# A GNN stack: a fill of a spare tile ahead of each group's gathers, and the spline weights moved from PSUM to SBUF

## The chip, the cores and the metric

The kernel runs on one core of one Trainium2 chip. The time is the device time of one execution in microseconds (us). The engines are PE (TensorE), DVE (VectorE), ACT (ScalarE), POOL (GpSimd) and SP (SyncE, which here only issues transfers).

## The reference, cut to what matters

A graph with N = 12500 nodes of 64 features and E = 200000 edges, sorted by destination, passes through four residual layers:

```python
h = relu(layernorm(x)); x = x + L0(h)  # spline convolution: every edge has 8 weights,
                                       # msg = sum_k w[e,k] * (h[src] @ W[k]); mean over dst; batch norm; elu
h = relu(layernorm(x)); x = x + L1(h)  # graph attention: softmax over the edges of a dst node of
                                       # leaky_relu(xl[src] + xr[dst]) @ att, weighted sum of xl[src]
h = relu(layernorm(x)); x = x + L2(h)  # three graph convolutions: normalised sum of h[src] over dst
h = relu(layernorm(x)); x = x + L3(h)  # mean of h[src] over dst, joined with h, one product
```

The 8 weights of an edge are the products of three pairs (1 - f, f), one pair for each of its three attributes.

## The kernel before, in words

The edge list is cut into 392 groups of 512 edges (J = 4 columns of 128). For a group, POOL issues four indirect transfers (L544). Each takes 128 row numbers from a column of `idx_block` in SBUF and brings 128 rows of a table in DRAM into one slot of the ring `gath`, which has S = 8 slots. PE then multiplies the rows with one-hot matrices, which sum them by destination tile (128 nodes). A group and tile pair is a visit; a group has one visit or a few.

The passes over the groups follow one another:

- The spline pass (`spline_tab`, 392 groups). DVE forms `hat2` (L1139, 16 columns), from it the 8 weights `hat8` (L1142, 32 columns), and then z = rows times weights (L1147, 2048 columns), which goes to SBUF. z reads the gathered rows from SBUF and `hat8` from PSUM. Then come the visits: DVE makes four one-hot tiles (L1118), PE multiplies (L800, L803, L808), DVE adds the results.
- The attention pass (`gat_tab`, 392 groups). Each visit is a chain over PE, DVE and ACT (L1258 makes its one-hot tile).
- Four sum passes (`sum_tab`, 168 groups each, 672 in all). Here the other 224 groups are covered by a dense matrix of edge counts: SP loads panels of it, and PE multiplies them (L909, L910) between the visits (L893). DVE makes the visits' one-hot tiles with L1343 (two inputs in SBUF) and adds the sums (L1324, L1327).

That dense matrix is filled on the way: 900 indirect accumulating transfers (L518, "scatters") are issued by POOL, 36 for every 28 groups, between the gathers of the spline pass from its 113th group on and of the attention pass. Each waits until the previous one has landed.

The order on POOL: before a group's first gather it waits until its slot is free (`slot_free`, L540). DVE gives a slot back at the end of a group (`free_slot`, L1051, an empty instruction), always that of four groups ago. So when group g is done, POOL may issue the gathers of group g + 4. Every 28 groups POOL copies the next row numbers (L503) and, where there are scatters, their cells and counts (L509, L510). POOL's sequencer handles waits ahead of the engine, so that instructions lie ready behind one another.

```python
pool.wait_ge(slot_free[s], pool_count)                       # 541
for j in range(J):
    nc.gpsimd.indirect_dma_start(out=dest[:, s, j, :], ...)  # 544, then_inc(gathered[s], 16)
    if cells and (j == J - 1 or j == 1 and hi - lo == 2):
        scatter(...)                                         # 518
```

Of the kernel before, what the change touches and what calls it, by code (L numbers as in the profile page):

```python
# [5 lines left out]
def gnn_stack_kernel(  # L6
# [19 lines left out]
    P = 128  # L26
# [3 lines left out]
    KS = W0.shape[0]  # L30
# [3 lines left out]
    J = 4  # L34
# [12 lines left out]
    NBLK = NG // BG  # L47
# [11 lines left out]
    NX = 1  # L59
# [22 lines left out]
    gat_tab = nc.dram_tensor("gat_tab", (T * P, 2 * F), fp32).ap()  # L82
    sum_tab = nc.dram_tensor("sum_tab", (T * P, 3 * F), bf16).ap()
# [6 lines left out]
    with ctx:  # L90
        def sb(name, shape, dt=fp32):
            return ctx.enter_context(nc.sbuf_tensor(name, shape, dt))
# [4 lines left out]
        def sem(name):  # L97
            return ctx.enter_context(nc.semaphore(name))
# [5 lines left out]
        R = sb("R", [P, T * F])  # L104
# [56 lines left out]
        o = 2 * J * KS * F  # L161
        zt = R[:, o:o + GE]
        o += GE
        hat2 = R[:, o:o + 4 * J].rearrange("p (j a b) -> p j a b", a=2, b=2)
        o += 4 * J
        cell_a, times_a = R[:, o:o + DP].bitcast(i32), R[:, o + DP:o + DP + DP // 2].bitcast(fp16)
        lists = [A[:, k * DC:(k + 1) * DC].bitcast(i32) for k in range(2 * TWIN + 1)]
        work = [R[:, k * DC:(k + 1) * DC] for k in range(5)] + [hT[:, (TWIN - 1) * P:(TWIN - 1) * P + DC]]
# [5 lines left out]
        o = SD * GE  # L174
# [8 lines left out]
        count_block = sb("count_block", [P, 2 * SB], fp16)  # L183
        dense_i = sb("dense_i", [1, 2], i32)
        fold = sb("fold", [P, F])
        floor = sb("floor", [P, 1])
        neg_max = sb("neg_max", [P, 1])
        diff = sb("diff", [P, 1])
# [27 lines left out]
        psCD = pb("psCD", 1024)  # L216
        psC, psD = psCD[:, 0:512], psCD[:, 512:1024]
        psE = pb("psE", 1024)
        hat8 = psB[:, 0:KS * J].rearrange("p (j a b) -> p j a b", a=2, b=4)
        ps_turned, ps_product = (psA, psB), (psCD, psE)  # L220


# [31 lines left out]
        zero_ready = sem("zero_ready")  # L254
        zeroed = sem("zeroed")
        cells_ready = sem("cells_ready")
        cells_moved = sem("cells_moved")
        cells_copied = sem("cells_copied")
        scattered = sem("scattered")
# [94 lines left out]
        def registers(eng, name, n):  # L354

            regs = [eng.alloc_register(f"{name}{k}") for k in range(n)]
            for r in regs:
                eng.reg_mov(r, 0)
            return regs
# [120 lines left out]
        def _(pool):  # L480
# [39 lines left out]
                    in_=count_block[:, c:c + 1], in_offset=None, compute_op=ALU.add,  # L520
                ).then_inc(scattered, 16)

            def edge_loop(table, dest, first, last, cells=None):

                block0 = cells[2] if cells else 0
                with pool.Fori(first, last) as i:
                    for h in range(2):
                        for k in range(BG):
                            s = (h * BG + k) % S
                            if k == S:  # L530

                                copy_block(1 - h, i * 2 + (h + 1))
                                if cells:
                                    copy_cells(cells[0], cells[1], (block0 + h + 1) % 2, i * 2 + (block0 + h + 1))
                            pool.reg_add(pool_count, pool_uses, (h * BG + k) // S + 1)
                            if s >= LAG:
                                pool.reg_add(pool_count, pool_count, pool_early)
                            pool.wait_ge(loaded_edges, 16 * 9)
                            pool.wait_ge(block_copied, pool_copied)
                            pool.wait_ge(slot_free[s], pool_count)  # L540
                            lo, hi = k * SB // BG, (k + 1) * SB // BG
                            for j in range(J):
                                c = h * BC + k * J + j
                                nc.gpsimd.indirect_dma_start(  # L544
                                    out=dest[:, s, j, :], out_offset=None, in_=table,
                                    in_offset=bass.IndirectOffsetOnAxis(ap=idx_block[:, c:c + 1], axis=0),
                                ).then_inc(gathered[s], 16)
                                if cells and (j == J - 1 or j == 1 and hi - lo == 2):
                                    scatter((block0 + h) % 2 * SB + (hi - 1 if j == J - 1 else lo))
                    pool.reg_add(pool_uses, pool_uses, 2 * BG // S)  # L550
# [24 lines left out]
            pool.wait_ge(table_ready, 48)  # L575
            copy_block(0, 0)
            pool.reg_add(pool_early, pool_early, 1)
            edge_loop(gat_tab, gath_gat, 0, NBLK // 2, (cell_b, times_b, n + NX))
            _, first_block = dense_range(pool, "pool")
            with pool.Fori(0, 3) as layer:  # L580
                copy_block(0, first_block * 2)
                wait_apart(pool, pool_count, table_ready, layer * (16 * NS) + (48 + 16 * NS))
                pool.reg_add(pool_early, pool_early, 1)
                edge_loop(sum_tab, gath_sum, first_block, NBLK // 2)
            copy_block(0, first_block * 2)
            pool.wait_ge(table_ready, 48 + 4 * 16 * NS)
            pool.reg_add(pool_early, pool_early, 1)
            edge_loop(sum_tab, gath_sum, first_block, NBLK // 2)


        @block.scalar
# [366 lines left out]
        def _(dve):  # L958
# [62 lines left out]

            dve.wait_ge(rows_stored, 16)
            V.memset(A[P - 32:P, 2 * DC:(2 * TWIN + 1) * DC].bitcast(i32), FAR).then_inc(lists_clear, 1)
            for semaphore in slot_free + bc_free + [prod_t, prod_t] + panel_used + [dense_added, dense_folded]:
                V.engine_nop().then_inc(semaphore, 1)

            asked = [0]
# [435 lines left out]
```

## Time and profile before

| | us |
|---|---|
| median of 3 runs | 12690.88 |
| lowest and highest run | 12641.61, 12698.97 |
| the profiled execution: its own time | 12644.07 |
| its span | 12642.2 |
| PE busy | 8810.2 (70%) |
| POOL busy | 7247.4 (57%) |
| DVE busy | 4847.3 (38%) |
| ACT busy | 1810.1 (14%) |

The spline pass lies at 136 to 3835 us of the span, the attention pass at 4091 to 7668, and the sum passes at 7846 to 8955, 9066 to 10174, 10279 to 11379 and 11468 to 12569. Busy time leaves out waits, register work and the sequencers. Idle time of an engine is put down to what ended it: "DVEq L1051" is a slot given back, "issue" is idle time for which no event shows, and "remote" or "another core or an unknown queue" is an event whose source the profile can't name.

### The profile page before, as it was taken

Reading aid. Unit: us, or ns where it says so; the run is one execution under the profiler, and the core shown is the slowest. Engines: PE = TensorE matmul, PEld = TensorE weight load, DVE = VectorE, ACT = ScalarE, POOL = GpSimd, SP = SyncE. Lnnn points to the kernel's source line nnn. Section 1 sums busy time; section 2 is a strip of 40 time slices with the busy share of each in tenths; the row PEclk is TensorE's granted clock in tenths of the full one; section 3 lists DMA queues with packets and bytes.
Section 4 is the critical chain, followed back from the end, with each engine's and each line's share of the span. In section 5 each row is a group of like instructions: output and inputs, shape, how many; then the busy total and the mean of one; then the engine's idle time right before and its main releaser. Section 6 shows DMA issues by size and latency. Waiting matters only on the chain.

```text
span 12642.2 us, 197864 instructions
## 1 busy us (share of the span) xinstructions
PE 8810.2 (70%) x46558; PEld 6095.1 (48%) x46559; DVE 4847.3 (38%) x11847; ACT 1810.1 (14%) x4731; POOL 7247.4 (57%) x6848
## 2 busy tenths in 40 slices
PE   4787777778784666666667764788378747864885
PEld 4787777777774444555555553222222222221222
DVE  5554444444446233333333334222322232234223
ACT  0000000000001233333333332000000000000000
POOL 3446665655554776666666662556455545664664
PEclk8888888888886677777777786888588868876887
DMA  7401111111111322222222221444244424433443
GB/s 286 155 17 14 14 13 13 13 13 13 12 12 25 62 61 60 59 60 58 57 56 56 56 54 38 146 148 150 57 149 151 137 77 146 154 115 105 149 153 90
DMA packets 577485, 1013.05 MB, mean 80 GB/s; under 512 B 342921, under 2 KB 352440, under 8 KB 577331
## 3 DMA queue, kind: packets, MB, share of 16 engines
q1 hardware_dynamic: 258819, 724.21, 17.0%
q0 software_dynamic: 316112, 286.92, 12.9%
q14 instruction: 138, 1.13, 0.0%
q10 hardware_dynamic: 2400, 0.53, 0.0%
q8 instruction: 16, 0.26, 0.0%
HBM read 862.36 MB, written 148.79 MB: 80 GB/s over the span
## 4 chain that ended last, share of the span: by engine, by line
PE 34%; another core or an unknown queue 31%; issue 15%; DVE 7%; DVEq 4%; DMA 3%; ACT 3%; SPq 1%; ACTq 1%; POOL 0%; POOLq 0%
PE psAB L800 13%; PE psCD L910 4%; PE psCD L909 4%; DMA R<-dense 2%; PE psCD L808 2%; PE psAB L853 2%; PE psCD L866 2%; PE psAB L859 1%; DVE one_hot L1118 1%; PE psCD L844 1%; ACT Q L702 1%; PE psAB L850 1%; PE psCD L781 1%; PE psAB L893 1%
## 5 line engine op out<-in xcount | busy, mean ns | idle before, releaser
L544 POOL DMA_INDIRECT gath<-sum_tab,idx_block x2688 | 2669.2, 993 | 2201.8 <-issue 1154.8
L800 PE MATMUL psAB<-one_hot,R 128*128 128x128 f32 x15680 | 2424.4, 316 | 633.6 <-DVE one_hot L1118 317.0
L800 PEld LDWEIGHTS psAB<-one_hot,R 128*128 128x128 f32 x15680 | 2254.6, 221 | 707.7 <-issue 658.2
L544 POOL DMA_INDIRECT gath<-spline_tab,idx_block x1568 | 1502.0, 958 | 1542.0 <-DVEq L1051 1058.1
L544 POOL DMA_INDIRECT gath<-gat_tab,idx_block x1568 | 1541.2, 983 | 1023.2 <-DVEq L1051 579.7
L909 PE MATMUL psCD<-R,Q 128*128 128x512 f16 x3528 | 1505.2, 427 | 563.3 <-DMA R<-dense 493.7
L518 POOL DMA_INDIRECT dense<-count_block,cell_block x900 | 1496.3, 1663 | 424.2 <-issue 268.8
L910 PE MATMUL psCD<-R,Q 128*64 128x512 f16 x3528 | 1555.3, 441 | 17.2 <-issue 17.1
L1343 DVE SCALAR_TENSOR_TENSOR R<-iota_row,tile_base,dstf 128x512 f32 x928 | 705.1, 760 | 1168.3 <-issue 1168.3
L893 PE MATMUL psAB<-gath,R 128*128 128x192 bf16 x3712 | 508.2, 276 | 822.7 <-DVE R L1343 406.6
L1324 DVE TENSOR_REDUCE row_part<-psAB 128x64 f32 x940 | 331.7, 353 | 1855.9 <-PE psAB L893 756.8
L1118 DVE TENSOR_SCALAR one_hot<-iota_row,tile_base,dstf 128x128 fp32r<-128x128 f32 x1952 | 602.7, 354 | 1115.8 <-remote 676.5
L909 PEld LDWEIGHTS psCD<-R,Q 128*128 128x128 bf16 x3528 | 343.5, 97 | 1424.7 <-issue 1424.0
L1263 DVE CUSTOM_DVE_ANT_0 Q<-psAB,Q 128x512 f32<-128x512 f32 x492 | 340.0, 691 | 1548.6 <-remote 1110.0
L866 PEld LDWEIGHTS psCD<-gath,Q 128*128 128x128 f32 x3936 | 597.5, 222 | 686.2 <-issue 685.8
L1147 DVE TENSOR_TENSOR R<-gath,psAB 128x2048 f32<-128x2048 f32 x392 | 896.2, 2286 | 18.6
L910 PEld LDWEIGHTS psCD<-R,Q 128*64 128x64 bf16 x3528 | 387.1, 110 | 962.4 <-issue 962.4
L850 PE MATMUL psAB<-one_hot,xr_hi 128*128 x492 | 301.1, 612 | 782.5 <-ACT xr_lo L691 420.9
L866 PE MATMUL psCD<-gath,Q 128*128 x3936 | 589.1, 300 | 308.6 <-issue 171.4
L893 PEld LDWEIGHTS psAB<-gath,R 128*128 x3712 | 311.7, 101 | 1015.8 <-issue 996.3
L853 PEld LDWEIGHTS psAB<-ident,gath 128*128 128x128 f32 x3936 | 714.1, 255 | 65.8 <-issue 0.5
L853 PE MATMUL psAB<-ident,gath 128*128 128x128 f32 x3936 | 709.4, 340 | 0.3 <-issue 0.3
(252 smaller groups left out, 9263.1 us busy)
## 6 DMA issues: line engine op xcount, KB each, us to landing
R<-dense SPq DMA_DIRECT2D x504, 896.0 KB
dense<-stage SPq DMA_DIRECT2D x126, 896.0 KB
Q<-dst_rows SPq DMA_DIRECT2D x392, 256.0 KB
gath<-sum_tab,idx_block POOLq DMA_INDIRECT x2688
gath<-spline_tab,idx_block POOLq DMA_INDIRECT x1568
gath<-gat_tab,idx_block POOLq DMA_INDIRECT x1568
sum_tab<-Q SPq DMA_DIRECT2D x28, 672.0 KB, 5.5
dense<-count_block,cell_block POOLq DMA_INDIRECT x900
```

Of the source, the lines that this page charges most:

```text
L518: nc.gpsimd.indirect_dma_start(out=dense, out_offset=bass.IndirectOffsetOnAxis(ap=cell_block[:, c:c + 1], axis=0), in_=count_block[:, c:c ...
L544: nc.gpsimd.indirect_dma_start(out=dest[:, s, j, :], out_offset=None, in_=table, in_offset=bass.IndirectOffsetOnAxis(ap=idx_block[:, c:c + ...
L800: nc.tensor.matmul(block, z[:, w, j, k * P:(k + 1) * P], oh32[:, j, :], start=(j == 0), stop=(j == J - 1))
L850: nc.tensor.matmul(psA[:, pair], xr_hi[:, :], onehot, start=True, stop=False)
L853: ins = nc.tensor.matmul(psA[:, bass.ds((v & 1) * GE + j * P, P)], gath_gat[:, s, j, :], ident[:, :], start=False, stop=(j == J - 1))
L866: ins = nc.tensor.matmul(psD[:, 0:F], prT[:, j * P:(j + 1) * P], gath[:, bass.ds(o + j * P, F)], start=(j == 0), stop=(j == J - 1))
L893: ins = nc.tensor.matmul(psAB[:, ring(v, 0, SV, 512, 3 * F)], oh16[:, bass.ds((v & (SV - 1)) * GE + j * P, P)], gath_sum[:, s, j, :], star ...
L909: nc.tensor.matmul(psC, tile[:, 0:2 * F], counts, start=first_one, stop=last_one)
L910: ins = nc.tensor.matmul(psD[0:F, :], tile[:, 2 * F:3 * F], counts, start=first_one, stop=last_one)
L1118: V.tensor_scalar(oh32r[:, j, :], iota_row[:, :], tile_base[:, bass.ds(t, 1)], dstf[:, bass.ds(chunk_col + j, 1)], ALU.add, ALU.is_equal). ...
L1147: V.tensor_tensor(z[:, s % 2, :, :].rearrange("p j (k f) -> p j k f", f=F), gath_spline[:, s, :, :].unsqueeze(2).to_broadcast([P, J, KS, F ...
L1343: V.scalar_tensor_tensor(oh16[:, ring(v, 0, SV, GE)].rearrange("p (j n) -> p j n", j=J), iota_row[:, :].unsqueeze(1).to_broadcast([P, J, P ...
```

## The change

- A new tile `spacer` (128 x 256, fp32, SBUF) and a semaphore `spacer_set`, which starts at 1.
- In the attention pass and the sum passes POOL fills this tile with zeros once per group, after the wait for the slot and before the group's four gathers. It waits first for the fill of the group before (`spacer_set` against a register that counts up). The tile is read by nobody.
- `hat8` moves from PSUM (`psB`) to SBUF (`R`, behind `hat2`); the lists behind it in `R` shift by 32 columns.

```diff
-        o += 4 * J
+        hat8 = R[:, o + 4 * J:o + 12 * J].rearrange("p (j a b) -> p j a b", a=2, b=4)
+        o += 12 * J
...
+        spacer = sb("spacer", [P, 256])
...
-        hat8 = psB[:, 0:KS * J].rearrange("p (j a b) -> p j a b", a=2, b=4)
...
+        spacer_set = sem("spacer_set")
...
+            (pool_spaced,) = registers(pool, "pool_spaced", 1)
+
-            def edge_loop(table, dest, first, last, cells=None):
+            def edge_loop(table, dest, first, last, cells=None, spaced=False):
...
                             lo, hi = k * SB // BG, (k + 1) * SB // BG
+                            if spaced:
+                                pool.reg_add(pool_spaced, pool_spaced, 1)
+                                pool.wait_ge(loaded_edges, 16 * 9)
+                                pool.wait_ge(spacer_set, pool_spaced)
+                                nc.gpsimd.memset(spacer[:, :], 0.0).then_inc(spacer_set, 1)
...
-            edge_loop(gat_tab, gath_gat, 0, NBLK // 2, (cell_b, times_b, n + NX))
+            edge_loop(gat_tab, gath_gat, 0, NBLK // 2, (cell_b, times_b, n + NX), spaced=True)
...
-                edge_loop(sum_tab, gath_sum, first_block, NBLK // 2)
+                edge_loop(sum_tab, gath_sum, first_block, NBLK // 2, spaced=True)
...
-            edge_loop(sum_tab, gath_sum, first_block, NBLK // 2)
+            edge_loop(sum_tab, gath_sum, first_block, NBLK // 2, spaced=True)
...
-            for semaphore in slot_free + bc_free + [prod_t, prod_t] + panel_used + [dense_added, dense_folded]:
+            for semaphore in slot_free + bc_free + [prod_t, prod_t] + panel_used + [dense_added, dense_folded, spacer_set]:
                 V.engine_nop().then_inc(semaphore, 1)
```

## Rows read from the trace of the kernel before

**Rows 1.** The page: busy time by engine, and the shares of the chain by engine.

```profile
PE 8810.2 (70%) x46558; PEld 6095.1 (48%) x46559; DVE 4847.3 (38%) x11847; ACT 1810.1 (14%) x4731; POOL 7247.4 (57%) x6848
...
PE 34%; another core or an unknown queue 31%; issue 15%; DVE 7%; DVEq 4%; DMA 3%; ACT 3%; SPq 1%; ACTq 1%; POOL 0%; POOLq 0%
```

**Rows 2.** Windows of two passes: length, busy us of PE, PEld, DVE, ACT, POOL.

```profile
136.00:3835.00 3699.00, 2901.42 (x21437) 2806.28 (x21438) 1804.16 (x4123) 338.75 (x976) 2094.95 (x1965) 0.85 0.19 45
...
7846.00:8955.00 1109.00, 796.29 (x2824) 285.71 (x2824) 296.25 (x686) 9.65 (x18) 669.74 (x679) 0.80 0.43 133
```

**Rows 3.** Windows of line L1147 (z) alone: DVE busy (count).

```profile
200.00:900.00 700.00, 210.34 (x92) 0.88 0.39 145
1000.00:3800.00 2800.00, 633.49 (x278) 0.84 0.12 13
```

**Rows 4.** Waits of POOL, 1000 to 3800: us in total, times, longest.

```profile
POOL gath L544 <- DVEq L1051: 742.0, 179, 11.2
```

**Rows 5.** The page: gathers of the three kinds of pass, busy us, mean ns | idle before.

```profile
L544 POOL DMA_INDIRECT gath<-sum_tab,idx_block x2688 | 2669.2, 993 | 2201.8 <-issue 1154.8 <-DVEq L1051 958.0 <-DMA sum_tab<-Q 89.0
...
L544 POOL DMA_INDIRECT gath<-spline_tab,idx_block x1568 | 1502.0, 958 | 1542.0 <-DVEq L1051 1058.1
L544 POOL DMA_INDIRECT gath<-gat_tab,idx_block x1568 | 1541.2, 983 | 1023.2 <-DVEq L1051 579.7 <-issue 411.0 <-DMA dense<-count_block,cell_block 31.7
```

**Rows 6.** Line L544: who waited for its gathers (us, times).

```profile
  PE psAB L893: 240.7, 15
  PE psCD L844: 25.5, 1
```

**Rows 7.** DVE groups by form: busy us, mean ns | idle before.

```profile
L1147 DVE TENSOR_TENSOR R<-gath,psAB 128x2048 f32<-128x2048 f32 x392 | 896.2, 2286 | 18.6
...
L1142 DVE TENSOR_TENSOR psAB<-Q,R 128x32 f32<-128x32 f32 x392 | 79.0, 202 | 55.9 <-issue 0.2
...
L1139 DVE TENSOR_TENSOR R<-Q 128x16 f32 x392 | 68.4, 175 | 179.8 <-issue 179.7
...
L1039 DVE TENSOR_TENSOR R<-X,s 128x6272 f32<-128x6272 f32 x4 | 26.8, 6692 | 0.1
...
L1387 DVE TENSOR_TENSOR H<-R,Q 128x896 f32<-128x896 f32 x21 | 22.5, 1085 | 0.4
```

**Rows 8.** Timeline, start of the attention pass: start us, us, engine, line.

```profile
4091.74 1.04 POOL L544 DMA_INDIRECT gath<-gat_tab,idx_block  x1 [0.80 <-POOL idx_block L503]
4092.01 6.69 DVE L1228 TENSOR_TENSOR R<-R,H 128x6272 f32<-128x6272 f32 x1 [5.55 <-ACT H L615]
4093.08 6.47 POOL L544 DMA_INDIRECT gath<-gat_tab,idx_block  x1 [0.30 <-issue]
```

**Rows 9.** Timeline, one group of the spline pass: z and the first gather.

```profile
2059.93 2.29 DVE L1147 TENSOR_TENSOR R<-gath,psAB 128x2048 f32<-128x2048 f32 x1
2059.95 0.98 POOL L544 DMA_INDIRECT gath<-spline_tab,idx_block  x1 [0.69 <-issue]
```

**Rows 10.** Line L492: the only fill of 128 x 256 on POOL.

```profile
L492 POOL MEMSET hT<- x1: 313/313/313, 2.1 to 2.1; 128x256 f32 x1
```

**Rows 11.** Timeline of POOL, second sum pass: a copy queued behind a gather.

```profile
9480.55 0.29 POOL L503 COPY idx_block<-srci 128x112 int32 x1
```

**Rows 12.** Timeline of POOL, attention pass: a copy and the gather behind it.

```profile
5128.49 0.79 POOL L510 COPY count_block<-Q 128x36 f16 x1
5129.75 1.01 POOL L544 DMA_INDIRECT gath<-gat_tab,idx_block  x1 [0.47 <-issue]
```

**Rows 13.** Waits of PE in 7846 to 7880, the head of the first sum pass.

```profile
PE psAB L893 <- DMA gath<-sum_tab,idx_block: 47.8, 4, 34.8
```

**Rows 14.** Line L1258 (attention pass): ns min/median/max.

```profile
L1258 DVE TENSOR_SCALAR one_hot<-Q,node_no x488: 485/486/848, 4113.7 to 7661.6; 128x512 f32 x163
```

**Rows 15.** Line L1343 (two inputs in SBUF, sum passes): ns min/median/max.

```profile
L1343 DVE SCALAR_TENSOR_TENSOR R<-iota_row,tile_base,dstf x928: 750/751/822, 7840.7 to 12572.8; 128x512 f32 x186
```

**Rows 16.** Waits of DVE, 1000 to 3800.

```profile
DVE one_hot L1118 <- remote: 528.2, 233, 8.4
```

## The prediction

> **What bounds the kernel now.** I read the busy times first, then the chain that ended last, then windows of the passes, and last the waits of POOL and of those who need its gathers. PE is busy 70% of the span and is the largest single part of the chain, with 34%; the next is 31% of events without a known source, then 15% "issue". POOL, the engine that the change loads, is busy 57% and has 0% of the chain [rows 1]. So what counts is how much idle time POOL has in each pass, and whether anybody waits for gathers.
>
> In the spline pass POOL is busy 2095 of 3699 us, in the first sum pass 670 of 1109 [rows 2]. With scatters running, z comes every 2800/278 = 10.1 us, before them every 700/92 = 7.6 us [rows 3]. In the stretch with scatters POOL waited 742.0 us for a slot given back, 742.0/278 = 2.67 us per group [rows 4]. In the sum passes it waited 958.0 us over 672 groups, 1.43 us each; in the attention pass 579.7 us over 392 groups, 1.48 us each [rows 5]. These three are POOL's slack. In the whole span PE waited for a gather 16 times [rows 6], and z stood idle before its start for 18.6 us over 392 groups, with no gather named [rows 7]. The gathers run ahead: group g + 4 is issued when g is done, so three whole groups (some 30 us with scatters) lie between issue and use.
>
> **The change, part by part.**
>
> *hat8 in SBUF, the instructions themselves.* L1142 writes 32 columns to PSUM in 202 ns; L1139 writes 16 columns to SBUF in 175 ns. The slope of a product with both inputs in SBUF is (6692 - 1085)/(6272 - 896) = 1.043 ns per column [rows 7], so 16 columns more make 192 ns: 10 ns saved, 392 times, on DVE's path, -4 us. At most it falls to 175 ns, -11 us; at least it stays, 0. z: from the same two rows, 2048 columns with all inputs in SBUF would take 1085 + 1152 x 1.043 = 2287 ns; it takes 2286 ns now [rows 7]. So 0; a start held by a running gather is bounded below.
>
> The Trainium skill says otherwise: its page "Perfetto Trace Analysis", section "Optimizing Scalar/DVE Operations", gives a DVE operation about 60 ns of access overhead on SBUF and about 125 ns on PSUM. By it both instructions would lose 65 ns, an estimate of 392 x 2 x 0.065 = 51 us saved. The row of z bears out none of that, and I go by the row.
>
> *hat8 in SBUF, what it does to POOL.* Now z has one input in SBUF; afterwards it has two. What two do is seen at the start of the attention pass: L1228, both inputs in SBUF, ran from 4092.01 for 6.69 us; a gather begun at 4093.08, inside it, took 6.47 us where its neighbour, begun before it, took 1.04 [rows 8]. The gather ended at 4099.55, 0.85 us after L1228, so it was held at a point about 0.1 us behind its start (0.96, the mean of the spline pass [rows 5], less 0.85). Beside z it isn't held now: a gather begun 0.02 us after z took 0.98 us [rows 9]. Afterwards it will be: it waits until z ends, 2.29 - 0.02 - 0.10 = 2.17 us. POOL issues in order, so one z holds one instruction of POOL: at most 2.17 us a group, at least 0 (POOL idle). Where POOL comes from one gather to the next every 1.25 us, the mean is nearer 2.17 - 0.6 = 1.6. I take 1.6 and keep 2.17 as the bound. Both are below the slack of 2.67 us, so POOL still waits for slots, and 30 us lie between issue and use against 7.4 (its 10.07 us per group less 2.67) + 2.17 of work, which leaves 20 us for the landing: z has its rows in time. Cost on the path: 0. The cover gone, it would be what exceeds 2.67, times 280 groups.
>
> The page "SBUF — State Buffer" of the Trainium skill, section "Who interferes with whom", states the same contention (two SBUF inputs on DVE against a GpSimd instruction that reads SBUF), and that issue order decides who blocks. By the second half z could be the one held; that is the first rival below.
>
> *The fill.* POOL gets 392 + 672 = 1064 fills of 128 x 256. The one such fill in the trace took 0.31 us [rows 10]. A copy behind a gather starts with no gap [rows 11]; from the end of a copy (5129.28) to the gather behind it is 0.47 us [rows 12], where gather to gather is 0.30 [rows 8]. So a fill adds 0.31 to 0.48 us; the short copies queued beside others took 0.79 [rows 12], which is my upper bound. The register wait is for a fill long done, and the sequencer handles it ahead. I take 0.45 us: 479 us more work for POOL. Behind the fill in POOL's queue are the group's four gathers and the scatters; for the gathers waits PE.
>
> In the attention pass 0.45 stands against a slack of 1.48, and PE waited once for a gather: 0. In the sum passes it stands against 1.43. There it shows only where PE lives from hand to mouth: at the head of each pass, where POOL starts from nothing and PE waits for each of the first four groups [rows 13]. The fourth is late by four fills: 4 x 0.45 = 1.8 us per pass, 7 us in four passes (5 to 13 by the bounds). Behind it the dense panels keep PE busy and POOL catches up.
>
> *The fill against DVE.* L1258 takes 486 ns, but up to 848: it is sometimes held, as I take it by an instruction of POOL, the held gather the other way round [rows 14]. A fill of 0.31 us falls on it in about (0.49 + 0.31)/7.3 = 11% of visits (the pass's 3577 us over 488 visits are 7.3), half of it lost: 392 x 0.11 x 0.2 = 9 us at most, 0 at least; I take 4. L1343 varies by 72 ns at most over 928 times [rows 15]: 0.
>
> *Sum.* -4 + 0 + 7 + 4 = +7 us, against the profiled execution's own 12644.07 (span 12642.2 and 1.9 around it). That execution is 0.4% below the median of the runs, 12690.88; put on the median, 12,698.
>
> **The rivals.**
>
> *z is held by the gathers (slower).* Place: L1147. If z can't start while an instruction of POOL is running, it waits for its rest. POOL is busy 57% of the spline pass [rows 2], and half of a gather or scatter is about 0.55 us: 0.57 x 0.55 = 0.31 us per z, 392 x 0.31 = 123 us: 12,821. For it: L1258's 848 ns [rows 14]. Against it: L1343, which has two inputs in SBUF as z will have, ran 928 times beside a POOL busy 60% [rows 2] and never took more than 822 ns, median 751 [rows 15]. It decides from 63/392 = 0.16 us per z on.
>
> *The fill is dear (slower).* If wait, fill and restart of the gathers come to 1.6 us, more than the slack, POOL becomes the bound: (1.6 - 1.43) x 672 + (1.6 - 1.48) x 392 = 161 us: 12,859. Against it are all rows of fills and copies.
>
> *The unknown stalls move.* Between 1000 and 3800 DVE waited 528 us in one of its lines for events without a source [rows 16], and a group costs 10.1 - 7.6 = 2.5 us more than before the scatters, 280 times, 700 us [rows 3]. Whatever disturbs the engines runs beside POOL's transfers. The held gathers move out of z into the time between groups, and the fills spread the gathers. If a tenth of the 700 us goes, -70 us: 12,628; if a tenth comes on top, 12,768. No row says which.
>
> *The change does nothing*, since z isn't in the way of a gather: the time stays as forecast, and only the trace shows it.
>
> **How the numbers follow.** Forecast (with the case that nothing happens) 58%; z held 12%; fill dear 5%; stalls fewer 15%; stalls more 10%. About 0.5%, 63 us, is what a measurement can tell from no change. Faster: 15%. Within: 58%. Slower: 12 + 5 + 10 = 27%. The range 12,620 to 12,830 takes in the bounds of the sum (-11 to +33 us), both cases of moved stalls and a held z, and leaves out the dear fill and worse.
>
> **What would show it.** hat8: L1142 at 175 to 202 ns, z at 2286 ns; slower than 2350 speaks for the first rival. Gathers of the spline pass: the mean up from 958 ns to about 958 + 1600/4 = 1360, with single ones above 3 us, and POOL's wait for slots in 1000 to 3800 down from 742 us to about 300. If that wait is near zero and z waits for gathers, the cover was thinner than I reckon. Fills: 1064 at 0.31 us, POOL's wait for slots down by about 0.45 us per group in the later passes, PE's waits for gathers still at the heads only. A change of any pass's length by over 60 us proves the sum wrong.

## The result: faster by 3.35% where the forecast said no change

| | before | after |
|---|---|---|
| median, us | 12694.67 (4 runs) | 12253.02 (4 runs) |
| lowest, highest | 12641.61, 12698.97 | 12229.47, 12295.55 |
| profiled execution: span | 12642.2 | 12293.6 |

The ratio is 0.9665, 95% interval 0.9627 to 0.9704. The forecast was 12,698 us and its range ended at 12,620.

Later jobs put the kernel before at 12,444, 12,629, 12,422, 10,209 and 12,439 us. Numbers of different jobs are compared here as ratios to the kernel before in the same job, or as passes of kernels of one job. The fourth job turned the verdict round: there the same change ran at 1.0687. Both signs have to be explained.

The page after, busy time and the chain's shares, answers to [rows 1]:

```profile
PE 8694.3 (71%) x46558; PEld 6005.2 (49%) x46559; DVE 4817.1 (39%) x11847; ACT 1804.7 (15%) x4731; POOL 8130.3 (66%) x7912
...
another core or an unknown queue 28%; PE 24%; issue 13%; DVE 5%; DMA 3%; DVEq 3%; ACT 3%; ACTq 1%; SPq 1%; POOL 0%; POOLq 0%
```

POOL has 883 us more work, and the kernel ends 349 us earlier in the profiled executions. Windows of the changed kernel (columns as in [rows 2]): the spline pass, a stretch inside it, the first sum pass.

```profile
135.00:3451.00 3316.00, 2760.68 (x21433) 2697.31 (x21434) 1774.44 (x4126) 338.33 (x974) 2631.79 (x1965) 0.90 0.21 50
1000.00:3400.00 2400.00, 1991.02 (x15271) 1942.71 (x15270) 1206.24 (x2872) 241.06 (x694) 1946.65 (x1429) 0.89 0.14 15
7455.00:8572.00 1117.00, 798.46 (x2836) 290.44 (x2836) 298.92 (x697) 9.65 (x18) 724.04 (x846) 0.79 0.43 132
```

The spline pass, 3699 us before [rows 2], is 383 us shorter: all of the gain and more. PE does the same instructions there in 2761 us in place of 2901, at a granted clock of 0.90 in place of 0.85: it spends more of the pass at the upper of its two levels. The attention pass ran 3559 us (before 3577), the sum passes 1117, 1108, 1128 and 1127 (1117, 1113, 1107 and 1106). A pass is measured here in every kernel from its first gather to the last work on its own groups; for the first sum pass before that gives 8 us more than the window of [rows 2].

The groups of the page after that answer to [rows 5], [rows 7] and [rows 10], and the fills:

```profile
L553 POOL DMA_INDIRECT gath<-spline_tab,idx_block x1568 | 1973.9, 1259 | 629.0 <-issue 536.7
...
L553 POOL DMA_INDIRECT gath<-gat_tab,idx_block x1568 | 1528.9, 975 | 456.7 <-issue 441.4
...
L550 POOL MEMSET spacer<- 128x256 f32 x1064 | 483.9, 455 | 1647.2 <-DVEq L1060 1165.9
...
L1156 DVE TENSOR_TENSOR R<-gath,R 128x2048 f32<-128x2048 f32 x392 | 900.1, 2296 | 437.4 <-DMA gath<-spline_tab,idx_block 423.2
```

The gathers are held as forecast (958 ns before, 1259 now), and z isn't. But z now waits 423.2 us for its rows, and POOL hardly waits for slots any more. Who waited in 1000 to 3400 us of the spline pass, before:

```profile
POOL gath L544 <- DVEq L1051: 620.6, 152, 11.2
DVE one_hot L1118 <- remote: 475.0, 205, 8.4
...
DVE A L1126 <- remote: 268.6, 114, 4.2
```

and after:

```profile
DVE R L1156 <- DMA gath<-spline_tab,idx_block: 379.5, 106, 6.7
...
DVE one_hot L1127 <- remote: 154.8, 94, 7.5
...
DVE A L1135 <- remote: 101.4, 51, 4.1
...
POOL gath L553 <- DVEq L1060: 24.6, 10, 3.4
```

The two waits "remote" fell from 744 to 256 us. They are what the change took away, and the waits for gathers are the largest of DVE's waits now.

**What such a wait is.** The timeline of the kernel before, one visit (start, us, engine, line):

```profile
2004.11 0.95 POOL L544 DMA_INDIRECT gath<-spline_tab,idx_block  x1 [0.30 <-issue]
...
2005.01 1.13 DVE L1118 TENSOR_SCALAR one_hot<-iota_row,tile_base,dstf 128x128 fp32r<-128x128 f32 x4
2005.01 1.08 PE L808 MATMUL psCD<-w_spline,R 128*128 128x64 f32 x8
2005.37 1.62 POOL L518 DMA_INDIRECT dense<-count_block,cell_block  x1 [0.30 <-issue]
...
2007.29 0.99 POOL L544 DMA_INDIRECT gath<-spline_tab,idx_block  x1 [0.30 <-issue]
2008.21 0.22 DVE L1126 TENSOR_TENSOR A<-A,psCD  x1 [2.07 <-remote]
2008.28 0.17 ACT L660 ACTIVATE edge_count<-psE  x1 [6.00 <-remote]
```

L1126 adds what L808 made. L808 ended at 2006.09 and DVE was free at 2006.14; the addition starts at 2008.21. PE meanwhile went on with the next visit's products (L800 from 2005.93 on). PE's release reached DVE some 2 us late, while POOL issued one transfer behind the other. I call this a late release. The trace also records the update of the semaphore itself: in the late visits it lies 0.33 us ahead of L1126 (median). So the delay is between PE's product and the update, as far as the profile's modelled ends of the products can tell.

To count them I took from each trace, for every visit with scatters running (from 1000 us to the end of the spline pass), the time from the later of "L808 done" and "DVE's previous operation done" to the start of L1126 (0.15 to 0.2 us is the mean where nothing is late; "over 1 us" is late, and the median of the late ones before is 2.1 us):

```
kernel, in the order of the text          visits  sum us  mean us  over 1 us
before                                     373     387     1.04     42%
after                                      359     165     0.46     18%
hat8 in SBUF alone (e1)                    357     131     0.37     17%
late fills alone: spline pass as before    371     308     0.83     42%
gathers behind z (e3)                      384     307     0.80     30%
one fill of 1280 per group (e4)            363     103     0.28     12%
four fills of 320 (e6)                     366      71     0.19      3%
wait for landing (e7)                      380     382     1.00     44%
four fills on one partition (e11)          367     113     0.31     13%
four tiny fills (e16)                      372     303     0.81     38%
all passes split (e10)                     358      56     0.16      1%
job at 10,209 us: tiny fills (e12)         338      69     0.20      0%
job at 10,209 us: the change (e15)         352      54     0.15      0%
```

This is one wait of several in a visit, so the sums are a gauge, not the whole cost.

When a release is late shows if the same visits are sorted by what POOL was doing at the moment that DVE could have gone on. "Paused" means more than 0.4 us behind the end of POOL's last transfer. The other columns give the time since the first transfer behind such a pause. A transfer that is held (a gather of over 1.2 us, a scatter of over 1.9) counts as a pause until 0.96 us before its end. The numbers are late visits of all:

```
kernel                              paused     under 2 us    2 to 4 us     over 4 us
before                             0 of 163      7 of 9      77 of 114     71 of 84
wait for landing (e7)              0 of 150     10 of 16     72 of 109     85 of 102
gathers behind z (e3)              0 of 96       6 of 134     5 of 30     106 of 121
one fill of 1280 per group (e4)    0 of 69       0 of 159    11 of 70      31 of 62
after                              0 of 7        0 of 230     2 of 30      62 of 89
four fills of 320 (e6)             2 of 31      10 of 278     0 of 54         none
four fills on one partition (e11)  4 of 33      39 of 144     1 of 132      2 of 55
job at 10,209 us: e12              0 of 4        0 of 10      0 of 2        0 of 319
```

In the first five rows nothing is late with POOL paused, and over 4 us into a train 50 to 88% of the visits are (before has too few under 2 us to tell). In `after` 98% of the gaps between two transfers are the usual 0.30 us, so the pause that counts there lies inside the held gather. The rule isn't sharp: in e11 visits under 2 us are late too, and in the 112 groups ahead of the scatters e4 has 15 late of 30 under 2 us.

### The profile page after: what moved, and what is told of

Read it like the earlier page. It is cut to its first block, busy times and chain, and to the rows that moved or that the text cites. A ratio compares the mean times of both kernels' runs of the same rounds, so it can differ in the third digit from the quotient of the medians.

```text
span 12293.6 us, 201058 instructions
## 1 busy us (share of the span) xinstructions
PE 8694.3 (71%) x46558; PEld 6005.2 (49%) x46559; DVE 4817.1 (39%) x11847; ACT 1804.7 (15%) x4731; POOL 8130.3 (66%) x7912
## 4 chain that ended last, share of the span: by engine, by line
another core or an unknown queue 28%; PE 24%; issue 13%; DVE 5%; DMA 3%; DVEq 3%; ACT 3%; ACTq 1%; SPq 1%; POOL 0%; POOLq 0%
PE psAB L809 5%; PE psCD L919 4%; PE psCD L918 4%; DMA R<-dense 3%; PE psAB L862 2%; PE psCD L875 1%; PE psAB L868 1%; ACT Q L711 1%; PE psCD L817 1%; PE psCD L853 1%; PE psAB L783 1%; PE psCD L790 1%; PE psE L790 1%; PE psAB L859 1%
## 5 line engine op out<-in xcount | busy, mean ns | idle before, releaser
L809 PE MATMUL psAB<-one_hot,R 128*128 128x128 f32 x15680 | 2318.7, 309 | 480.2 <-DVE one_hot L1127 374.3
L809 PEld LDWEIGHTS psAB<-one_hot,R 128*128 128x128 f32 x15680 | 2170.2, 214 | 528.2 <-issue 503.7
L553 POOL DMA_INDIRECT gath<-spline_tab,idx_block x1568 | 1973.9, 1259 | 629.0 <-issue 536.7
L520 POOL DMA_INDIRECT dense<-count_block,cell_block x900 | 1549.6, 1722 | 418.4 <-issue 272.4
L550 POOL MEMSET spacer<- 128x256 f32 x1064 | 483.9, 455 | 1647.2 <-DVEq L1060 1165.9
L1156 DVE TENSOR_TENSOR R<-gath,R 128x2048 f32<-128x2048 f32 x392 | 900.1, 2296 | 437.4 <-DMA gath<-spline_tab,idx_block 423.2
```

Source lines behind the costliest of these rows:

```text
L520: nc.gpsimd.indirect_dma_start(out=dense, out_offset=bass.IndirectOffsetOnAxis(ap=cell_block[:, c:c + 1], axis=0), in_=count_block[:, c:c ...
L550: nc.gpsimd.memset(spacer[:, :], 0.0).then_inc(spacer_set, 1)
L553: nc.gpsimd.indirect_dma_start(out=dest[:, s, j, :], out_offset=None, in_=table, in_offset=bass.IndirectOffsetOnAxis(ap=idx_block[:, c:c + ...
L809: nc.tensor.matmul(block, z[:, w, j, k * P:(k + 1) * P], oh32[:, j, :], start=(j == 0), stop=(j == J - 1))
L1156: V.tensor_tensor(z[:, s % 2, :, :].rearrange("p j (k f) -> p j k f", f=F), gath_spline[:, s, :, :].unsqueeze(2).to_broadcast([P, J, KS, F ...
```

## The experiments

The theory at the end: where releases come late, they do so beside POOL's indirect transfers issued without a pause; a pause in the issuing, whether POOL is held or fills a tile in it, takes the lateness away from the visits just behind it. Rivals on the way: the freed PSUM, no gather beside z, the fills' writes, any instruction between two transfers.

**The two parts alone (first job; before 12,444 us).** e1 takes the first hunks of the diff, e2 the rest.

```diff
-        hat8 = psB[:, 0:KS * J].rearrange("p (j a b) -> p j a b", a=2, b=4)
+        hat8 = R[:, o + 4 * J:o + 12 * J].rearrange("p (j a b) -> p j a b", a=2, b=4)
```

> Only hat8 moves to SBUF, no fills. The spline pass of the changed kernel was 382 us shorter, the later passes together were a few tens of us longer. If the move of the weights carries the whole gain (all three theories below say so), this kernel is at about 12,694 - 440 = 12,250 to 12,260, with a spline pass of about 3,316 us, and is not slower than the changed kernel. If the fills carry part of it, it is clearly above 12,300. Theories on why the move helps: (beside) POOL's transfers no longer run beside z and the turn of the group behind it; (PSUM) z no longer reads PSUM for 2.3 us; (pace) POOL as a whole is slower and its transfers come later.

> Only the fills, hat8 stays in PSUM. By the prediction's sum the fills cost 7 us at the heads of the sum passes and up to 9 by holding L1258: 12,700. If the fills spread the gathers to advantage, it is below 12,640. The spline pass has none and stays at 3,700 us.

e1: 12113.91 us, ratio 0.9742 (0.9701 to 0.9784), spline pass 3297 us against 3643 in e2, whose spline pass is the one of before. e2: 12348.05 us, 0.9929 (0.9906 to 0.9952), attention pass 3409 us against 3457 to 3465 in the three others of the job. The product of both, 0.967, is the whole change: the parts are independent, and three quarters come from `hat8`.

**Gathers kept away from z (first job).** `hat8` stays in PSUM; POOL issues the gathers of group g + 4 only when z of group g + 1 is done, and no longer as soon as group g is.

```diff
+                            if behind_z:
+                                pool.reg_add(pool_z, pool_z, 1)
+                                pool.wait_ge(loaded_edges, 16 * 9)
+                                pool.wait_ge(z_ready, pool_z)
```

> The kernel before (hat8 in PSUM, no fills), but POOL issues the first gather of a group of the spline pass only when z of the next group is done, not when the slot is given back 0.7 us ahead of z. So the first gather of a group that waited for its slot doesn't run beside z, with no port in play. (beside): most of the 382 us of the spline pass go. (PSUM): nothing goes, 3,700 us stay, or the pass is a little longer, since gathers come 2.5 us later. (pace): a part goes.

12573.99 us, 1.0119 (1.0076 to 1.0163), spline pass 3790 us. POOL waited for z, and DVE no less for late releases (before: 475.0 us in the same stretch):

```profile
POOL gath L550 <- DVE R L1153: 632.5, 127, 14.7
DVE one_hot L1124 <- remote: 620.8, 349, 9.2
```

That the first gathers no longer overlap with z isn't the gain.

**One long fill per group in the spline pass (first job).** `hat8` stays in PSUM.

```diff
+                                nc.gpsimd.memset(one_hot[:, GE:GE + 1280].bitcast(fp32), 0.0).then_inc(spacer_set, 1)
...
-            edge_loop(spline_tab, gath_spline, 0, S0)
+            edge_loop(spline_tab, gath_spline, 0, S0, spaced=True)
```

> The kernel before with hat8 in PSUM, and a fill of 1280 columns (about 1.2 us, as much as z held POOL per group in the changed kernel) ahead of each group's gathers in the spline pass alone. POOL is as slow as in the changed kernel, but its transfers run beside z as before. (pace): the spline pass falls towards 3,316 us. (PSUM): it stays near 3,700. (beside): it stays near 3,700, or falls by the part of first gathers that the fill moves out of z (the fill starts with z and takes half of it).

12139.47 us, 0.9761 (0.9719 to 0.9803), spline pass 3341 us. A fill that nobody reads does nearly what `hat8` in SBUF did (e1: 3297 us), with 1.465 us per group where the hold in e1 cost (1278 - 958) x 4 = 1.28. So neither the place of `hat8` nor z's own speed is needed for the gain; what both edits have in common is a pause in POOL's train.

**The kernel before against itself (second job; before 12,629 us).**

> The kernel before, unchanged, profiled on this chip, as the base for the lengths of the passes. Ratio 1.00. The runs so far left one theory (breaks): while POOL issues indirect transfers without a break for more than some 2 us, PE's signals reach the other engines late; a break lets them through. By it, the first line to look at is the wait of DVE's L1118 for events without a source, 676 us in the profile of before.

1.0008 (0.9991 to 1.0025); spline pass 3704, attention pass 3595, sums 1107 to 1111 us.

**Four short fills (second job).** The 1280 columns in four, one ahead of each gather.

```diff
+                                if spaced:
+                                    at = GE + j * 320
+                                    nc.gpsimd.memset(one_hot[:, at:at + 320].bitcast(fp32), 0.0).then_inc(spacer_set, 1)
```

> hat8 in PSUM, spline pass only: the 1280 columns of fill of the run before are cut into four fills of 320, one ahead of each gather. POOL gets the same extra work, some 1.3 us per group, but no gap between two transfers is longer than about 0.9 us. (pace): as good as one fill of 1280, a ratio of 0.976. (breaks, one long one needed): less, 0.98 to 1.00. (breaks, what counts is the share of time in transfers): as good or better.

12200.92 us, 0.9652 (0.9628 to 0.9676), spline pass 3220 us: 484 us shorter than e5. Late releases nearly vanish, and z waits for gathers:

```profile
DVE R L1157 <- DMA gath<-spline_tab,idx_block: 388.2, 126, 6.1
...
DVE one_hot L1128 <- remote: 51.1, 54, 4.6
```

**A pause between groups, not between transfers (second job).** `hat8` stays in PSUM, and in the spline pass POOL waits until the gathers of the group before have landed.

```diff
+                            if landed and p >= 0:
+                                if p % S == 0:
+                                    pool.reg_add(pool_landed, pool_landed, 16 * J)
+                                pool.wait_ge(loaded_edges, 16 * 9)
+                                pool.wait_ge(gathered[p % S], pool_landed)
```

> hat8 in PSUM, no fills, spline pass only: POOL issues a group's gathers only when those of the group before have landed. So every group's four gathers are a run of their own, with a pause of some 2 us behind it in which POOL does nothing. (breaks): the pause is as good as a fill, the spline pass falls to about 3,340 us, ratio 0.975. If only work on POOL helps, or if it is the port, the ratio is 1.00. If it makes POOL the bound (5 + 2.5 + 2 us per group against 10), the pass is at 3,500 to 3,700 with z waiting for gathers.

12673.06 us, 1.0029 (1.0011 to 1.0048), spline pass 3718 us, late releases as before (505.4 us):

```profile
DVE one_hot L1126 <- remote: 505.4, 225, 8.7
```

The edit didn't bring the pause that it was meant to bring. With scatters running POOL paused over 0.4 us ahead of 213 of 284 groups, 773 us in all, where e5 did so ahead of 213 of 277, 804 us in all: the wait for the landing took the place of the wait for the slot. So e7 shows that transfers still under way don't matter, but not whether an idle pause does what a fill does. Nor is it the sum of the pauses that counts: e4 has only 493 us of them and few late releases. There the fill moved the train: 228 of 360 visits fell into a pause or its first 2 us, in e7 166 of 377.

**Longer fills in the later passes (second job; e9 in the third, before 12,422 us).** The change with 704 columns in place of 256, then the same in four parts.

```diff
-        spacer = sb("spacer", [P, 256])
+        spacer = sb("spacer", [P, 704])
```

```diff
+                                if spaced:
+                                    nc.gpsimd.memset(spacer[:, j * 176:(j + 1) * 176], 0.0).then_inc(spacer_set, 1)
```

> The changed kernel with fills of 704 columns instead of 256 in the attention and sum passes, about 0.7 us in place of 0.31 to 0.45. (breaks): longer breaks free more of the stalls while POOL still has slack there (1.4 us per group), 20 to 100 us less than the changed kernel's ratio of 0.967. (fills only cost): 4 passes x 4 groups x 0.3 us and more, a few us to some tens slower than 0.967.

> hat8 in SBUF as in the changed kernel; in the attention and sum passes the 704 columns of the long fill are cut into four fills of 176, one ahead of each gather of the group. POOL's added work per group is about the same (4 x about 0.4 us against about 1.0). Theory (unbroken trains of POOL's transfers make the other engines' releases late, and every gap counts): spreading the gaps helps more than one gap per group; ratio to before 0.92 to 0.935 against 0.938 with one long fill, attention pass below 3301 us. Rival (what helps is that POOL has less idle time or is held back once per group, however it is spread): 0.938 +- 0.004. Rival (extra instructions of POOL cost by their number): above 0.945.

e8: 11868.46 us, 0.9384 (0.936 to 0.9409); attention pass 3301 us against 3595 in e5, sums 4336 against 4438. e9: 11744.52 us, 0.9468 (0.9442 to 0.9493); attention pass 3235 against 3445 in e11, sums 4232 against 4381. So the fills were far too short for what they could do, and the expectation for e9 was missed. The two ran in different jobs, so which form is better in the later passes isn't settled: each against a kernel of its job whose later passes are those of before, the split one saved less in the attention pass (210 us against 294) and more in the sum passes (149 against 102). Such unaltered passes differ within one job by up to 66 us over the four sum passes (e1, e3, e4), so the second difference says nothing.

**Fills that write almost nothing, and all passes split (third job).** e11 is e6 on one partition; e10 has `hat8` in PSUM and a fill ahead of every gather.

```diff
-                                    nc.gpsimd.memset(one_hot[:, at:at + 320].bitcast(fp32), 0.0).then_inc(spacer_set, 1)
+                                    nc.gpsimd.memset(one_hot[0:1, at:at + 320].bitcast(fp32), 0.0).then_inc(spacer_set, 1)
```

> The kernel with four short fills in the spline pass (ratio 0.965), each fill on one partition in place of 128: the same duration, 1/128 of the bytes written. Theory (the gap in time between transfers counts): 0.965 +- 0.004, spline pass about 3220 us. Rival (the fill's writes to SBUF, its lock of the port or its hold on DVE count): near 1.00, spline pass near 3700 us.

> hat8 stays in PSUM as before; one fill ahead of each gather everywhere: 320 columns in the spline pass, 176 in the attention and sum passes. Theory (gaps): spline pass about 3220 us as with the four short fills alone, attention pass as in the kernel with hat8 in SBUF and split fills; ratio about 0.925. Rival (hat8 in SBUF is needed for the gain in the attention pass too, or parts are not additive): above 0.945.

e11: 11912.66 us, 0.9592 (0.9566 to 0.9618), spline pass 3158 us. e10: 11630.46 us, 0.9371 (0.9349 to 0.9393), spline pass 3174 us, attention pass 3230. The spline pass of e11 is that of e10 with 1/128 of the bytes written in it, so the writes aren't what works; the pause between the transfers grew in both, from 0.30 us to 0.52 in e11 and 0.55 in e10 (median between two gathers). e4's one fill per group took 574 us of POOL's time in all, e11's four took 654: the spline pass is 3341 us with the one and 3158 with the other, at nearly the same time before (12,444 and 12,422). One pause per transfer does more than one per group, as far as two jobs can be compared.

**Tiny fills, and the later passes again (fourth job; before 10,209 us).**

```diff
-                                    nc.gpsimd.memset(one_hot[0:1, at:at + 320].bitcast(fp32), 0.0).then_inc(spacer_set, 1)
+                                    nc.gpsimd.memset(one_hot[0:1, at:at + 16].bitcast(fp32), 0.0).then_inc(spacer_set, 1)
```

> The kernel with four fills on one partition in the spline pass (0.959, fills of 417 ns), each cut from 320 columns to 16, so that it lasts some 100 ns. Theory (length of the gap between two transfers counts): the gap shrinks by about 0.3 us of about 0.5, so much less than the full gain: ratio 0.975 to 0.99, spline pass 3400 to 3600 us. Rival (any instruction of POOL's own between two transfers breaks the train, its length does not matter): 0.96, spline pass about 3160 us.

> The kernel with one fill of 704 columns per group in the attention and sum passes and hat8 in SBUF, again, beside the split one on the same chip. Theory (every gap counts): about 0.955 here, slower than the split fills (0.947 on its chip) by 0.5 to 1.5%. Rival (the late passes gain by POOL's added time per group, not by the number of gaps): the same as the split kernel within 0.3%.

> The same with the 704 columns in four fills of 176, one ahead of each gather, again. Both theories: 0.947 as before if this is the same chip; the theory of gaps wants it below the kernel with the long fill, attention pass at 3235 us against 3300 or more, the rival wants them equal.

> The changed kernel unaltered, on the chip of the others. Its two parts alone came to 0.9742 and 0.9929 on one chip, product 0.967; both together 0.9665 on another. Parts independent: 0.967 +- 0.005 here too. If the parts get in each other's way or the gain depends on the chip: above 0.975 or below 0.96.

e12: 10225.08 us, 1.0014 (1.0004 to 1.0023). e13: 11303.34, 1.1073 (1.1054 to 1.1091). e14: 11258.45, 1.1028 (1.1009 to 1.1046). e15: 10907.92, 1.0687 (1.0669 to 1.0705). I had expected none of this. No late release shows in this job's traces; e12, which is the kernel before but for 356 us of tiny fills, shows the same step as above like this:

```profile
2000.14 1.62 POOL L519 DMA_INDIRECT dense<-count_block,cell_block  x1 [0.30 <-issue]
...
2001.70 1.14 DVE L1128 TENSOR_SCALAR one_hot<-iota_row,tile_base,dstf 128x128 fp32r<-128x128 f32 x4
2001.71 1.08 PE L818 MATMUL psCD<-w_spline,R 128*128 128x64 f32 x8
2002.07 0.99 POOL L554 DMA_INDIRECT gath<-spline_tab,idx_block  x1 [0.27 <-issue]
...
2003.14 0.22 DVE L1136 TENSOR_TENSOR A<-A,psCD  x1 [0.30 <-PE psCD L818]
```

The product is done at 2002.79, DVE is free at 2002.84, the addition starts at 2003.14. The windows of z in the stretch with scatters, e12 and e15 (DVE busy, count):

```profile
1000.00:2800.00 1800.00, 539.35 (x236) 0.95 0.16 17
```

```profile
1000.00:3300.00 2300.00, 579.98 (x253) 0.88 0.14 15
```

A group takes 1800/236 = 7.63 us without the change and 2300/253 = 9.09 with it. POOL never waits for a slot in either stretch: it sets the pace, and each held gather costs its full length (mean 966 ns in e12, 1290 in e15). The tiny fills of e12 cost no pace, since they fit into the 0.30 us between two transfers. e14 took 45 us less than e13, but where nothing is late this doesn't test the theory of gaps. The spline pass is 3260 us against 2781, +479; the attention pass 3089 against 3020; the sum passes 3571 against 3441. Together +678 us, of 676 between the two spans.

**The repetition (fifth job; before 12,439 us).**

> Four fills of 16 columns on one partition in the spline pass, again. If the kernel before takes about 10,210 us here, as beside the last runs (no late releases at all in the trace), the ratio is 1.00 again and nothing is told. If it takes 12,400 to 12,700 us (late releases): theory (the length of the gap counts) 0.975 to 0.99; rival (any instruction between two transfers is enough) 0.96.

> The changed kernel. Theory (the change gains only where releases come late, since it takes them away, and costs where they do not): 1.069 where the kernel before takes 10,210 us, 0.967 to 0.975 where it takes 12,400 to 12,700 us. Rival (the ratios differ for another reason, as the chip's number): 0.967 or 1.069 whatever the kernel before takes.

> One fill ahead of each gather everywhere, hat8 in PSUM. Where the kernel before takes 12,400 to 12,700 us: 0.93 to 0.937, with spline pass near 3170 us. Where it takes 10,210 us POOL sets the pace of nearly all passes and the fills cost their full length: about 2781 + 392 x 4 x 0.4 = 3400 us would be the most for the spline pass, with the time at 1.09 to 1.12 of before.

e16, the tiny fills: 12397.15 us, 0.9976 (0.9956 to 0.9996), spline pass 3633 us, and late releases are there again (its waits, 1000 to 3400):

```profile
DVE one_hot L1128 <- remote: 522.6, 206, 8.5
```

The group of its fills on the page:

```profile
L552 POOL MEMSET one_hot<- 1x16 f32 x1568 | 268.0, 171 | 888.3 <-DVEq L1061 810.8
```

An instruction of 171 ns between two transfers does almost nothing (a smaller gain than the 0.975 to 0.99 expected), one of 417 ns gave 4%. The trace shows why: from the end of one gather to the start of the next it is 0.30 us without fills and still 0.30 with the tiny ones (medians), against 0.52 in e11. The tiny fill adds no pause at all. So the rival "any instruction is enough" is refuted, and how the gain grows with the added pause wasn't measured between 0.30 and 0.52 us. e17, the change: 11978.54 us, 0.9646 (0.962 to 0.9672). Against e16, whose other passes are those of before, the spline pass is 339 us shorter, the attention pass 89, the sums 20 (within the spread of unaltered sum passes). e18: 11637.79 us, 0.9368 (0.9349 to 0.9387), the fastest kernel where releases come late, as e10 was. It wasn't run where they don't; there the kernel before is the fastest that I saw.

## Why the prediction was wrong

**What held.** L1142's successor took 196 ns against 202 (forecast 192), z 2296 against 2286 (forecast the same). By the figures of the Trainium skill (page "Perfetto Trace Analysis", section "Optimizing Scalar/DVE Operations") an operation would have lost 65 ns. The trace doesn't bear that out: 6 ns for one, none for the other. The hold: POOL was busy or issuing 2400 - 620.6 = 1779 us for 241 groups before, 7.38 us each, and 2375 us for 264 after, 9.00; the difference of 1.6 us is what I took. Of it some 1.2 us lie in the gathers ((1259 - 958) x 4; the forecast mean of 1360 was too high), the rest in held scatters and copies. The Trainium skill (page "SBUF — State Buffer", section "Who interferes with whom") states this contention; the trace agrees in that the gathers rose to 1259 ns. That issue order decides who blocks did not show: 331 of 392 times z began while a transfer of POOL was running, and it never took more than 2.36 us. This refutes the first rival, z held by gathers. The fills took 0.455 us (taken 0.45), and the first sum pass kept its 1117 us. L1258 rose from 249.3 us in all to 255.3, +6 for a forecast 4. PE's wait for gathers at the head of the first sum pass was 48.0 us after 47.8 [rows 13]: the +7 us were not there; why wasn't looked into. One sum of the prediction is off, and nothing hangs on it: the bounds of its parts add up to -6 and +22 us, not to -11 and +33.

**The step that failed** is "Cost on the path: 0" for the held gather together with the price of "the unknown stalls move". I had the mechanism in one sentence ("whatever disturbs the engines runs beside POOL's transfers; the held gathers ... spread the gathers"), gave it 15%, and sized it as a tenth of 700 us. Where the forecast had 0 and the rival 70 us, it measured 383 us in the spline pass of the first pair, 346 between e2 and e1, 339 between e16 and e17.

**How it was mis-sized.** The 700 us (10.1 less 7.6 us per group) were the wrong base. The stretch with scatters has more visits per group (367 for 279 groups against 120 for 112), and per visit it costs 7.65 us against 7.21. What was to be had stood in other rows: the wait "remote" of [rows 16], 528 us in one line, its like at L1126 (268.6 us), and the time that PE lost at a lower clock beside it. And the tenth had no row at all. A bound from above could have been worked out: POOL needs 7.4 us per group; with 1.6 of hold, 9.0. If all stalls went, the pass would fall from 10.08 us per group to POOL's pace, by 1.1 us, some 300 us in 280 groups. It took 9.08 us per group, and e15, where there are no late releases, 9.09. So with scatters running the gain is about as large as POOL lets it be. The 112 groups ahead of the scatters gave the rest: 7.66 us each before, 6.69 after. For them I had reckoned no stalls at all.

**The cover.** "z has its rows in time" (20 us to spare) failed too: z waited 423.2 us. (The prediction had named this as its sign: a wait for slots near zero and z waiting for gathers.) The slack of 2.67 us was itself made by the stalls. Once they went, POOL was behind, not ahead, and the lead of three groups was used up. I had reckoned the slack of an engine at the pace of before and not asked what is left of it if the pace rises. For the fourth job this is the whole story: the slack is 0, and the change costs 1.46 us per group there, about the hold.

**The chances.** 58% for no change rested on hidden POOL work. For the jobs with late releases that is wrong by 3.4 to 3.5%, and for the one without by as much as 6.9% the other way.

**Open.** Why releases come late in five jobs and not in one. It isn't the chip by its number: three jobs, at 12,444, 12,422 and 10,209 us before, ran on the same one. By which path POOL's transfers delay PE's releases, the records don't show. One difference stands beside the times: the traces of the fast job hold 147,225 to 150,467 recorded semaphore updates each, all others 57,186 to 68,053, though the kernels are in part the same to the letter (e12 147,562, e16 59,050). Whether updates go unrecorded because something delays them, or whether the recording has a part in the delay, no run tells; that rival is open. And which fill length is best in each pass wasn't searched.

## What to carry to other kernels

Idle time that ends in "remote" or "issue" while POOL issues one indirect transfer behind the other is a cost that may be removable by spacing the transfers: put fills of 0.4 to 0.5 us between them, see in the trace that the pause really grew (0.17 us left it at 0.30), and look whether the wait goes. Before relying on it, time the kernel in several jobs: if one of them is much faster than the others, a change that spaces the transfers may lose there what it wins elsewhere. And the slack of an engine holds only for the pace at which it was read: put its own work per group beside the pace that the change hopes for.

## What the runs showed of the hardware

- In the jobs with late releases, PE's release reached DVE up to 4.2 us after the product (42% of visits over 1 us with transfers in trains, median of these 2.1 us; 3% with some 0.5 us between most transfers). With POOL paused it was never late (0 of 163), over 4 us into a train in 71 of 84 visits. In the job without them, trains that ran for tens of us delayed nothing (no visit over 1 us of 338 and 352), and the kernel before took 10,209 us, 18 to 20% less.
- Fills of 171 ns between transfers left the pause at 0.30 us and gave 0.2%; of 417 ns (pause 0.52 us) 4.1%; of 517 ns (0.54 us) 3.5%, each in a job of its own.
- A DVE operation with two inputs in SBUF held gathers, which then took up to 3.1 us (median 948 ns, mean 1259), and did not become slower itself.
